# Group maxima spread by fp32r products of diagonals, and the group variances by one fp32r record, in a linear-attention kernel

## The chip, the cores and the metric

The kernel runs on one core of one Trainium2 chip. A core has TensorE (PE: matmuls; PEld: its weight loads), VectorE (DVE), ScalarE (ACT), GpSimd (POOL) and SyncE (SP: the DMA queue here). The metric is the device time of one execution in microseconds (us), lower is better.

## The reference

Sixteen images of 64x64 pixels with 256 channels. Each gets a group norm (32 groups of 8 channels), a linear attention with a softmax of k over the 4096 pixels, an output projection and a residual:

```python
g = x.reshape(16, 64, 64, 32, 8)                          # group norm, no affine part
x_n = (g - mean(g, (1, 2, 4))) / sqrt(var(g, (1, 2, 4)) + 1e-5)
q, k, v = split(einsum('bhwc,cd->bhwd', x_n, W_qkv), 3)   # each to b, channel, pixel
k = softmax(k, axis=-1)                                   # over the 4096 pixels
context = einsum('bdn,ben->bde', k, v)
out = einsum('bde,bdn->ben', context, q)
x + einsum('bhwc,cd->bhwd', out, W_out) + b_out
```

All of it is fp32. The kernel gets fp32 accuracy out of the faster fp32r products by splitting an operand into a high part (rounded to fp32r) and a low part (the rest), and adding the products of both.

## The kernel before

An image is 8 chunks of 512 pixels; CB = 2 halves of 128 channels; x comes in twice, channels on the partitions (xt) and pixels on the partitions (x). The group norm is folded into the weights: wk is scaled by rstd, and the shift of k by the mean drops out of the softmax. For each image: **keys** (k for each chunk, pixels on the partitions, in PSUM; ACT copies it to e_raw, VectorE keeps the running maximum mx of each channel); **exponentials** of k minus a maximum; **gather** (products of the exponentials with x, 8 chunks); **combine** (the 256x256 matrices with wq and wv wo); **emit** (that matrix times xt, plus bias, 8 chunks). TensorE interleaves: in period b it gathers image b, combines it, and then alternates emit of image b with keys of image n = b + 1. Written by hand, each engine's program is a fixed order, unrolled over the 16 images; semaphores (wait_ge, then_inc) tie them together. An engine works in order, so an instruction that waits holds all that is behind it.

The maximum is taken over two **blocks** of four chunks. For each block: `turn_max` (PE transposes mx, channels to the partitions), `block_max` (DVE reduces along the row to m_blk, one maximum for each channel), `spread_max` (PE brings the maxima back as a row on all partitions: the stationary operand is a column of m_blk broadcast to 128x128, the moving one the identity `ident`), `shift` (DVE subtracts that row from e_raw). `block_scales` computes dm, the difference between the block maxima and the whole one, from which ACT makes alpha. Block 0 of image n falls between the keys and emits of period b; block 1 of image b falls behind the first chunks of its own gather.

The statistics of image n are taken by VectorE in period b: BN_STATS on a copy of the input (xs), then `mean_of`: a product with the block matrix grp (1/8 inside a group) gives the group means of the per-channel means, and dev and var2 follow; `stats_var` on PE multiplies var2 by grp, `var_of` adds eps, POOL takes the power -1/2 (rstd), ACT scales wk with it. From image 2 on, both products stand in the gather of the image before, at block 1; image 1's stand later in image 0's gather. POOL makes the low parts: xt_lo and x_lo, each 128x1024 out of two tensors in SBUF. An fp32 product of the program shows in the trace as two records, an fp32r product as one.

The order on PE at block 1, in period b (stats_mean and stats_var for images from 2 on):

```python
gather_high(b, 0)
turn_max(b, 1)
if more and b:
    stats_mean(n)
gather_low(b, 0)
gather_high(b, 1)
spread_max(b, 1)
if more and b:
    stats_var(n)
gather_low(b, 1)
```

Of the kernel before, what the change touches and what calls it, by code (L numbers as in the profile page):

```python
# [31 lines left out]
def build(nc: bass.Bass, xt: bass.AP, xn: bass.AP, w: bass.AP, b_out: bass.AP, out: bass.AP):  # L32
# [11 lines left out]
    with ExitStack() as ctx:  # L44
        def sb(name, shape, dt=F32):
            return ctx.enter_context(nc.sbuf_tensor(name, shape, dt))
# [4 lines left out]
        def sem(name):  # L51
            return ctx.enter_context(nc.semaphore(name))
# [160 lines left out]
        def stats_psum(b, which):  # L213

            return ps_k[:, 0, 0, C + which * CB:C + (which + 1) * CB] if b == 1 else ps_k[:, 1, which, 0:CB]

        def max_psum(b, blk):

            return ps_e if b == 0 and blk == 0 else (ps_g0, ps_k[:, 0])[blk]
# [177 lines left out]
        def _(pe):  # L397
# [50 lines left out]
                last.then_inc(t_ps, 1)  # L448

            def spread_max(b, blk):  # L450

                to = max_psum(b, blk)
                pe.wait_ge(m_blk_ready, b * 2 + (blk + 1))
                for d in range(CB):
                    last = nc.tensor.matmul(to[:, 1, d * P:(d + 1) * P],
                                            m_blk[:, blk, d:d + 1].broadcast_to([P, P]), ident,
                                            start=(d == 0), stop=True, skip_group_check=True)
                last.then_inc(bc_ps, 1)

            def stats_mean(b):  # L460
                pe.wait_ge(mv_ready, b + 1)
                nc.tensor.matmul(stats_psum(b, 0), grp[:], mv[:, :, 0], start=True, stop=True).then_inc(mean_ps, 1)

            def stats_var(b):
                pe.wait_ge(var2_ready, b + 1)
                nc.tensor.matmul(stats_psum(b, 1), grp[:], var2[:], start=True, stop=True).then_inc(var_ps, 1)

            def gather_high(b, j):
                pe.wait_ge(e_hi_ready, b * NCH + (j + 1))
# [115 lines left out]
                emit_low(b, parity, *LATE[i])  # L585

            pe.wait_ge(consts_ready, 5)
            stats_mean(0)
            stats_var(0)
            pe.wait_ge(wvo_loaded, 32)  # L590
# [81 lines left out]
        def _(act):  # L672
# [165 lines left out]
        def _(dve):  # L838
# [19 lines left out]
            def mean_of(b, parity):  # L858
                dve.wait_ge(mean_ps, b + 1)
                nc.vector.tensor_tensor(dev[:], mv[:, :, 0], stats_psum(b, 0), ALU.subtract)  # L860
                nc.vector.tensor_scalar(neg_mean[:, parity, :], stats_psum(b, 0), -1.0, None,
                                        ALU.mult).then_inc(mean_read, 1)
                dve.wait_ge(mean_read, b + 1)
                for c in range(CB):
                    last = nc.vector.tensor_scalar(var2[:, c:c + 1], dev[:, c:c + 1], dev[:, c:c + 1], mv[:, c, 1:2],
                                                   ALU.mult, ALU.add)
                last.then_inc(var2_ready, 1)

            def var_of(b):
                dve.wait_ge(var_ps, b + 1)  # L870
                nc.vector.tensor_scalar(var_eps[:], stats_psum(b, 1), EPS, None, ALU.add).then_inc(var_eps_ready, 1)

            def wk_low(b, parity):
                dve.wait_ge(wk_hi_ready, b + 1)
# [23 lines left out]
            def block_max(b, blk):  # L898
                src = max_psum(b, blk)
                dve.wait_ge(t_ps, b * 2 + (blk + 1))  # L900
                nc.vector.tensor_reduce(m_blk[:, blk, :], src[:, 0, 0:C].rearrange("p (d n) -> p d n", d=CB),
                                        AX_X, ALU.max).then_inc(m_blk_ready, 1)

            def block_scales(b):
                dve.wait_ge(m_blk_ready, b * 2 + 2)
# [147 lines left out]
            def gather_steps(b, parity, more):  # L1053
                n, np_ = b + 1, 1 - parity
                block_max(b, 1)
                if more:
                    mean_of(n, np_)
                block_scales(b)
                mean_bias(b, parity)
                shift(b, 4)  # L1060
                if more:
                    var_of(n)
                e_low(b, 3)
                shift(b, 5)
# [86 lines left out]
```

## Time and profile before

| what | us |
|---|---|
| median of 3 runs | 1215.09 (1214.95 to 1216.85) |
| the profiled execution, its own time | 1214.93 |
| its span, first to last instruction | 1213.2 |
| PE busy | 1190.1 |
| PEld busy (overlaps PE) | 1115.8 |
| DVE busy | 842.1 |
| ACT busy | 840.1 |
| POOL busy | 622.4 |

The rows below come from the one profiled execution. A row of a timeline has the start in us from the span's start, the length in us (of all its xN instructions together), engine, line, operation, and out<-in by the program's names; in brackets the idle time before it and what ended it. Instructions of one engine are pipelined, so their records overlap; the distance between two starts tells what one costs. A name stands for its memory: m_blk is the block maxima, `zero_eye` holds the identity.

### The profile page before, as it was taken

What the parts mean: (1) busy time and instruction counts of PE and PEld (TensorE: products, weight loads), DVE (VectorE), ACT (ScalarE), POOL (GpSimd) and SP (SyncE); (2) the same over time, 40 slices, a digit from 0 to 9 for tenths busy, and PEclk for the clock granted to TensorE, in tenths of its full rate; (3) what the DMA queues carried; (4) which work ended last, traced back from release to release, by engine and by line L of the source; (5) the groups of instructions that cost most, each with busy time, mean ns of one, the idle gap of its engine ahead of it and who ended that gap; (6) DMA issues with size and microseconds to landing.
All of it is one profiled execution on the core that took longest, in us unless ns stands there. A gap on an engine that the chain in (4) does not pass through costs nothing.

```text
span 1213.2 us, 21447 instructions
## 1 busy us (share of the span) xinstructions
PE 1190.1 (98%) x8460; PEld 1115.8 (92%) x8460; DVE 842.1 (69%) x1582; ACT 840.1 (69%) x1140; POOL 622.4 (51%) x288
## 2 busy tenths in 40 slices
PE   4999999999999999999999999999999999999998
PEld 4998999999899998999989999899999989999897
DVE  6877667676776767768776677766767676676551
ACT  5767768677685776757677686776857768577664
POOL 8664564635645355563655636356463564536520
PEclk9999999999999999999999999999999999999999
DMA  9448666576765758666486665867657576573524
GB/s 339 146 167 294 218 235 205 195 269 208 274 203 199 264 172 294 226 206 237 162 301 229 221 227 183 286 209 252 204 201 263 193 278 225 201 252 122 191 74 170
DMA packets 107077, 266.71 MB, mean 220 GB/s; under 512 B 10208, under 2 KB 10208, under 8 KB 106976
## 3 DMA queue, kind: packets, MB, share of 16 engines
q1 hardware_dynamic: 106976, 265.33, 63.5%
q8 instruction: 67, 1.10, 0.4%
q14 instruction: 34, 0.28, 0.1%
HBM read 198.18 MB, written 67.11 MB: 219 GB/s over the span
## 4 chain that ended last, share of the span: by engine, by line
PE 93%; DVE 2%; ACT 1%; POOL 1%; DMA 1%; issue 1%; SPq 0%; DVEq 0%; POOLq 0%; ACTq 0%
PE ps_k L399 29%; PE ps_e L564 19%; PE ps_e L573 10%; PE ps_g L492 5%; PE ps_e L480 5%; PE ps_e L492 5%; PE ps_e L482 5%; PE ps_g L480 4%; PE ps_g L482 4%; PE ps_g L511 1%; PE ps_g L528 1%; PE ps_g L542 1%; PE ps_g L534 1%; POOL x_lo L347 1%; DVE mx L892 1%
## 5 line engine op out<-in xcount | busy, mean ns | idle before, releaser
L341 POOL TENSOR_TENSOR xt_lo<-xt_raw,xt_hi 128x1024 fp32r<-128x1024 f32 x128 | 307.4, 2404 | 434.5 <-ACT xt_hi L676 309.1
L347 POOL TENSOR_TENSOR x_lo<-x_raw,x_hi 128x1024 fp32r<-128x1024 f32 x128 | 281.4, 2216 | 65.6 <-ACT x_hi L681 56.2
L892 DVE TENSOR_TENSOR mx<-ps_k,mx 128x256 f32<-128x256 f32 x480 | 203.3, 424 | 95.8 <-ACT e_raw L685 74.3
L733 ACT ACTIVATE o_stage<-ps_e,bias 128x512 f32<-128x512 f32 x253 | 170.9, 689 | 114.1 <-PE ps_e L573 114.1
L399 PE MATMUL ps_k<-wk_hi,xt_hi 128*128 128x256 f32 x1024 | 207.1, 284 | 1.0 <-DVE mx L892 0.7
L399 PE MATMUL ps_k<-wk_lo,xt_hi 128*128 128x256 f32 x1024 | 205.5, 283 | 0.0
L685 ACT ACTIVATE e_raw<-ps_k 128x512 f32<-128x512 f32 x256 | 141.4, 596 | 87.2 <-PE ps_k L399 87.2
L849 DVE BATCH_NORM_STATS2 bn<-xs 128x6 f32<-128x512 f32 x240 | 154.5, 686 | 40.7 <-DMA xs<-in_xt_dram 39.5
L693 ACT ACTIVATE e_hi<-e_raw 128x1024 fp32r<-128x1024 f32 x128 | 135.1, 1055 | 60.9 <-DVE e_raw L917 33.0
L399 PEld LDWEIGHTS ps_k<-wk_hi,xt_hi 128*128 128x128 f32 x1024 | 163.4, 190 | 8.7 <-issue 1.8
L399 PE MATMUL ps_k<-wk_hi,xt_lo 128*128 128x256 f32 x1024 | 158.2, 283 | 0.0
L399 PEld LDWEIGHTS ps_k<-wk_lo,xt_hi 128*128 128x128 f32 x1024 | 157.4, 189 | 0.0
L564 PE MATMUL ps_e<-xt_hi,acc_hi 128*128 128x512 f32 x474 | 150.3, 398 | 0.0
L573 PE MATMUL ps_e<-xt_hi,u_lo 128*128 128x512 f32 x474 | 150.2, 398 | 0.0
L564 PE MATMUL ps_e<-xt_lo,acc_hi 128*128 128x512 f32 x474 | 148.8, 395 | 0.0
L681 ACT ACTIVATE x_hi<-x_raw 128x1024 fp32r<-128x1024 f32 x128 | 134.5, 1050 | 11.4 <-DMA x_raw<-in_xn_dram 11.2
L676 ACT ACTIVATE xt_hi<-xt_raw 128x1024 fp32r<-128x1024 f32 x128 | 135.0, 1055 | 3.8 <-DMA xt_raw<-in_xt_dram 3.8
L399 PEld LDWEIGHTS ps_k<-wk_hi,xt_lo 128*128 128x128 f32 x1024 | 137.3, 189 | 0.0
L480 PE MATMUL ps_e<-x_hi,e_hi 128*128 128x258 f32 x512 | 125.8, 283 | 0.7 <-POOL x_lo L347 0.7
L482 PE MATMUL ps_e<-x_lo,e_hi 128*128 128x256 f32 x512 | 125.5, 282 | 0.0
L482 PE MATMUL ps_g<-x_lo,e_hi 128*128 128x256 f32 x512 | 124.8, 281 | 0.0
L480 PE MATMUL ps_g<-x_hi,e_hi 128*128 128x258 f32 x512 | 124.8, 282 | 0.0
(129 smaller groups left out, 1992.7 us busy)
## 6 DMA issues: line engine op xcount, KB each, us to landing
xt_raw<-in_xt_dram SPq DMA_DIRECT2D x128, 512.0 KB, 4.3
x_raw<-in_xn_dram SPq DMA_DIRECT2D x128, 512.0 KB, 3.5
out_dram<-o_stage SPq DMA_DIRECT2D x127, 512.0 KB, 4.5
xs<-in_xt_dram SPq DMA_DIRECT2D x240, 256.0 KB, 5.1
w_setup<-in_w_dram SPq DMA_DIRECT2D x2, 256.0 KB, 10.1
out_dram<-o_stage SPq DMA_DIRECT2D x2, 256.0 KB, 2.0
wk<-in_w_dram SPq DMA_DIRECT2D x1, 256.0 KB, 9.9
wq_t<-in_w_dram SPq DMA_DIRECT2D x1, 256.0 KB, 10.9
```

Source lines behind the costliest of these rows:

```text
L341: nc.gpsimd.tensor_tensor(xt_lo[:, s], xt_raw[:, s], xt_hi[:, s].bitcast(F32), ALU.subtract).then_inc(xt_lo_ready, 1)
L347: nc.gpsimd.tensor_tensor(x_lo[:, s], x_raw[:, s], x_hi[:, s, :, 0:C].bitcast(F32), ALU.subtract).then_inc(x_lo_ready, 1)
L399: return nc.tensor.matmul(ps_k[:, j % 2, t // 2, (t % 2) * C:(t % 2 + 1) * C], (xt_hi, xt_lo)[xs_][:, slot(j, parity), c, t * P:(t + 1) * ...
L480: nc.tensor.matmul(ps_g[j // HALF][:, d, 0:C + 2], w_, x_hi[:, j % X_SLOTS, t, :], start=(j % HALF == 0 and t == 0), stop=False, skip_grou ...
L482: nc.tensor.matmul(ps_g[j // HALF][:, d, 0:C], w_, x_lo[:, j % X_SLOTS, t, :], start=False, stop=False, skip_group_check=True)
L564: nc.tensor.matmul(out_psum(b, u, h), hi[:, c, h * P:(h + 1) * P], x_[:, s, c, :], start=(n == 0 and c == 0), stop=False, skip_group_check ...
L573: last = nc.tensor.matmul(out_psum(b, u, h), lo[:, c, h * P:(h + 1) * P], xt_hi[:, s, c, :], start=False, stop=(c == CB - 1), skip_group_c ...
L685: nc.scalar.activation(e_raw[:, j, 2 * h:2 * h + 2, :].rearrange("p t c -> p (t c)"), ps_k[:, j % 2, h, :], ACT.Copy).then_inc(k_out, 1)
L693: nc.scalar.activation(e_hi[:, j % E_SLOTS], e_raw[:, j], ACT.Exp).then_inc(e_hi_ready, 1)
L733: nc.scalar.activation(o_stage[:, u % O_SLOTS, h, :], src, ACT.Identity, bias=bias[:, h:h + 1]).then_inc(o_ready, 1)
L849: nc.vector.bn_stats(bn[:, q % CB, q // CB, :], xs[:, q % S_SLOTS, :]).then_inc(bn_done, 1)
L892: nc.vector.tensor_tensor(mx[:], tile, mx[:], ALU.max).then_inc(max_done, 1)
```

## The change

From image 1 on, the spread multiplies a column of ones (`one_r`, broadcast to 128x128, fp32r) by a diagonal: VectorE builds diag_hi, the identity times m_blk rounded to fp32r, and diag_lo, identity times m_blk minus diag_hi (`block_diag`, right behind `block_max`), and PE adds two products of 256 columns. For the variances from image 1 on, VectorE splits var2 into a high and a low part side by side (var_parts), PE makes one fp32r product of 4 columns, and VectorE adds the two results. Image 0 keeps the fp32 products. grp becomes grp_r, an fp32r copy in the same memory that ACT writes at the start (1/8 and 0 are exact), and its fp32 products read it as fp32. The diagonals use the memory of u_hi, which is needed later in a period.

```diff
@@ tiles
-        grp = sb("grp", [P, P])
+        with nc.sbuf_tensor("grp", [P, P], F32) as grp:
+            pass
+        grp_r = sb("grp_r", [P, P], F32R)
+        one_r = sb("one_r", [P, 1], F32R)
+        var_sum = sb("var_sum", [P, CB])
+        var_parts = sb("var_parts", [P, 2, CB], F32R)
...
+        diag_hi, diag_lo = u_hi[:, 0, :], u_hi[:, 1, :]
@@ PE, spread_max
+                if b == 0:
...
+                else:
+                    pe.wait_ge(diag_hi_ready, (b - 1) * 2 + (blk + 1))
+                    nc.tensor.matmul(to[:, 1, 0:C], one_r[:].broadcast_to([P, P]), diag_hi, start=True, stop=False)
+                    pe.wait_ge(diag_lo_ready, (b - 1) * 2 + (blk + 1))
+                    last = nc.tensor.matmul(to[:, 1, 0:C], one_r[:].broadcast_to([P, P]), diag_lo,
+                                            start=False, stop=True)
@@ PE, stats_var
+                if b == 0:
...
+                else:
+                    pe.wait_ge(var_parts_ready, b)
+                    nc.tensor.matmul(var_psum(b), grp_r[:], var_parts[:].rearrange("p k c -> p (k c)"), start=True,
+                                     stop=True).then_inc(var_ps, 1)
@@ ACT, before its first chunk
+            act.wait_ge(consts_ready, 5)
+            nc.scalar.activation(grp_r[:], grp[:], ACT.Copy).then_inc(grp_r_ready, 1)
+            nc.scalar.activation(one_r[:], one_col[:], ACT.Copy).then_inc(one_r_ready, 1)
@@ DVE, end of mean_of
+                if b > 0:
+                    dve.wait_ge(var2_ready, b + 1)
+                    nc.vector.tensor_copy(var_parts[:, 0, :], var2[:]).then_inc(var_hi_ready, 1)
+                    dve.wait_ge(var_hi_ready, b)
+                    nc.vector.tensor_tensor(var_parts[:, 1, :], var2[:], var_parts[:, 0, :].bitcast(F32),
+                                            ALU.subtract).then_inc(var_parts_ready, 1)
@@ DVE, var_of
+                    nc.vector.tensor_scalar(var_sum[:], sums[:, 0:CB], EPS, None, ALU.add).then_inc(var_sum_ready, 1)
+                    dve.wait_ge(var_sum_ready, b)
+                    nc.vector.tensor_tensor(var_eps[:], sums[:, CB:2 * CB], var_sum[:],
+                                            ALU.add).then_inc(var_eps_ready, 1)
@@ DVE, new
+            def block_diag(b, blk):
+                if b == 0:
+                    return
+                dve.wait_ge(m_blk_ready, b * 2 + (blk + 1))
+                for d in range(CB):
+                    last = nc.vector.tensor_scalar(diag_hi[:, d * P:(d + 1) * P], ident, m_blk[:, blk, d:d + 1], None,
+                                                   ALU.mult)
+                last.then_inc(diag_hi_ready, 1)
+                dve.wait_ge(diag_hi_ready, (b - 1) * 2 + (blk + 1))
+                for d in range(CB):
+                    last = nc.vector.scalar_tensor_tensor(out=diag_lo[:, d * P:(d + 1) * P], in0=ident,
+                                                          scalar=m_blk[:, blk, d:d + 1],
+                                                          in1=diag_hi[:, d * P:(d + 1) * P].bitcast(F32),
+                                                          op0=ALU.mult, op1=ALU.subtract)
+                last.then_inc(diag_lo_ready, 1)
@@ DVE, gather_steps
                 block_max(b, 1)
+                block_diag(b, 1)
                 if more:
                     mean_of(n, np_)
@@ DVE, period
                 block_max(n, 0)
+                block_diag(n, 0)
                 bn_halves(8, 12)
```

PE at block 1 of an image from 1 to 14, behind the last products of gather_high(b, 1); before:

```order
L480 MATMUL ps_g0<-x_hi,e_hi 128x258
L482 MATMUL ps_g0<-x_lo,e_hi 128x256
L455 MATMUL ps_k<-zero_eye,m_blk 128x128 x2
L466 MATMUL ps_k<-var2,grp 128x2
L492 MATMUL ps_g0<-x_hi,e_lo 128x258 x8
```

The same place after the change (the lines of the program have moved: L512 and L514 are the old L480 and L482, L524 the old L492):

```order
L512 MATMUL ps_g0<-x_hi,e_hi 128x258
L514 MATMUL ps_g0<-x_lo,e_hi 128x256
L480 MATMUL ps_k<-u_hi,one_r 128x256
L482 MATMUL ps_k<-u_hi,one_r 128x256
L497 MATMUL ps_k<-var_parts,grp_r 128x4
L524 MATMUL ps_g0<-x_hi,e_lo 128x258 x8
```

The two fp32 products of the spread have become two fp32r products of double width, and the variance product has four columns; nothing else has moved there.

VectorE at the same block 1, from block_max to var_of; before:

```order
L901 TENSOR_REDUCE m_blk<-ps_k 128x2
L860 TENSOR_TENSOR dev<-mv,ps_k 128x2
L861 TENSOR_SCALAR neg_mean<-ps_k 128x2
L865 TENSOR_SCALAR var2<-dev,mv 128x1 x2
L906 TENSOR_REDUCE m_all<-m_blk 128x2
L909 TENSOR_TENSOR dm<-m_blk,m_all 128x4
L961 TENSOR_TENSOR b_mean<-b_col,neg_mean 128x2
L917 TENSOR_TENSOR e_raw<-e_raw,ps_k 128x1024
L871 TENSOR_SCALAR var_eps<-ps_k 128x2
```

After (L952 is the old L901, L897 to L902 the old L860 to L865, u_hi is the diagonals):

```order
L952 TENSOR_REDUCE m_blk<-ps_k 128x2
L960 TENSOR_SCALAR u_hi<-zero_eye,m_blk 128x128 x2
L965 SCALAR_TENSOR_TENSOR u_hi<-zero_eye,m_blk,u_hi 128x128 x2
L897 TENSOR_TENSOR dev<-mv,ps_k 128x2
L898 TENSOR_SCALAR neg_mean<-ps_k 128x2
L902 TENSOR_SCALAR var2<-dev,mv 128x1 x2
L907 CAST var_parts<-var2 128x2
L909 TENSOR_TENSOR var_parts<-var2,var_parts 128x2
L973 TENSOR_REDUCE m_all<-m_blk 128x2
L976 TENSOR_TENSOR dm<-m_blk,m_all 128x4
L1028 TENSOR_TENSOR b_mean<-b_col,neg_mean 128x2
L984 TENSOR_TENSOR e_raw<-e_raw,ps_k 128x1024
```

Four instructions stand between block_max and mean_of, and two more behind var2.

VectorE at block 0, behind the maxima of chunk 3; before:

```order
L892 TENSOR_TENSOR mx<-ps_k,mx 128x256 x4
L901 TENSOR_REDUCE m_blk<-ps_g0 128x2
L849 BN_STATS bn<-xs 128x6 x4
L917 TENSOR_TENSOR e_raw<-e_raw,ps_g0 128x1024
L889 COPY mx<-ps_k 128x256
```

After (L886 is the old L849, L984 the old L917):

```order
L943 TENSOR_TENSOR mx<-ps_k,mx 128x256 x4
L952 TENSOR_REDUCE m_blk<-ps_g0 128x2
L960 TENSOR_SCALAR u_hi<-zero_eye,m_blk 128x128 x2
L965 SCALAR_TENSOR_TENSOR u_hi<-zero_eye,m_blk,u_hi 128x128 x2
L886 BN_STATS bn<-xs 128x6 x4
L984 TENSOR_TENSOR e_raw<-e_raw,ps_g0 128x1024
```

The four instructions of the diagonals stand between block_max and the BN_STATS.

## Rows read from the trace of the kernel before

**Rows 1.** Page, busy time; then one image's window: us, busy us and instructions by engine, PEclk.

```profile
PE 1190.1 (98%) x8460; PEld 1115.8 (92%) x8460; DVE 842.1 (69%) x1582; ACT 840.1 (69%) x1140; POOL 622.4 (51%) x288
...
201.00:275.00 74.00, 74.00 (x531) 69.53 (x530) 52.77 (x100) 52.22 (x71) 38.35 (x18) 1.00 0.66 228
```

**Rows 2.** Waits of PE between 60 and 1150 us: total, times, longest.

```profile
PE ps_e L480 <- POOL x_lo L347: 0.7, 2, 0.4
```

**Rows 3.** Timeline of weight loads, block 1 (start, length, us).

```profile
498.64 0.53 PEld L455 LDWEIGHTS ps_k<-zero_eye,m_blk 128*128 128x128 f32 x4
499.09 0.30 PEld L466 LDWEIGHTS ps_k<-var,grp 128*128 128x128 f32 x2
499.31 1.02 PEld L492 LDWEIGHTS ps_g<-x_hi,e_lo 128*128 128x128 f32 x8
```

**Rows 4.** The same at block 0 of the next image.

```profile
546.12 1.02 PEld L399 LDWEIGHTS ps_k<-wk_hi,xt_lo 128*128 128x128 f32 x8
547.07 0.53 PEld L455 LDWEIGHTS ps_g<-zero_eye,m_blk 128*128 128x128 f32 x4
547.52 0.30 PEld L564 LDWEIGHTS ps_e<-xt_hi,acc_hi 128*128 128x128 f32 x2
```

**Rows 5.** Groups by form, VectorE: busy us, mean ns, idle before.

```profile
L876 DVE SCALAR_TENSOR_TENSOR wk_lo<-wk,rstd,wk_hi 128x256 fp32r<-128x256 f32 x32 | 13.9, 478 | 0.3 <-ACT wk_hi L708 0.3
```

**Rows 6.** Timeline of VectorE at block 1.

```profile
495.87 0.42 DVE L901 TENSOR_REDUCE m_blk<-ps_k 128x2 f32<-128x256 f32 x1 [1.71 <-PE ps_k L447]
496.21 0.15 DVE L860 TENSOR_TENSOR dev<-mv,ps_k 128x2 f32<-128x2 f32 x1
...
496.47 0.46 DVE L865 TENSOR_SCALAR var<-dev,mv 128x1 f32<-128x1 f32 x2
...
497.02 0.83 DVE L909 TENSOR_TENSOR dm<-m_blk,m_all 128x4 f32<-128x4 f32 x1
...
499.40 1.22 DVE L917 TENSOR_TENSOR e_raw<-e_raw,ps_k 128x1024 f32<-128x1024 f32 x1 [1.47 <-PE ps_k L455]
```

**Rows 7.** Timeline of VectorE at block 0.

```profile
544.54 0.42 DVE L901 TENSOR_REDUCE m_blk<-ps_g 128x2 f32<-128x256 f32 x1 [1.00 <-PE ps_g L447]
546.04 2.58 DVE L849 BATCH_NORM_STATS2 bn<-xs 128x6 f32<-128x512 f32 x4 [1.07 <-DMA xs<-in_xt_dram]
```

**Rows 8.** The tile dm: ns min/median/max over 16 images.

```profile
L909 DVE TENSOR_TENSOR dm<-m_blk,m_all x16: 161/833/849, 52.0 to 1158.7; 128x4 f32<-128x4 f32 x16
```

**Rows 9.** Timeline of GpSimd around block 1.

```profile
495.45 2.39 POOL L341 TENSOR_TENSOR xt_lo<-xt_raw,xt_hi 128x1024 fp32r<-128x1024 f32 x1 [7.59 <-ACT xt_hi L676]
500.77 1.60 POOL L357 TENSOR_TENSOR rstd<-var_eps,neg_half 128x2 f32<-128x2 f32 x1 [2.93 <-DVE var_eps L871]
```

**Rows 10.** Image 0: VectorE, then GpSimd.

```profile
55.31 2.79 DVE L924 TENSOR_TENSOR e_lo<-e_raw,e_hi 128x1024 fp32r<-128x1024 f32 x1
...
54.60 2.41 POOL L341 TENSOR_TENSOR xt_lo<-xt_raw,xt_hi 128x1024 fp32r<-128x1024 f32 x1
56.97 3.19 POOL L347 TENSOR_TENSOR x_lo<-x_raw,x_hi 128x1024 fp32r<-128x1024 f32 x1
```

**Rows 11.** Image 15: VectorE, then weight loads of PE.

```profile
1155.16 1.87 DVE L892 TENSOR_TENSOR mx<-ps_k,mx 128x256 f32<-128x256 f32 x4 [2.48 <-ACT e_raw L685]
...
1157.08 0.20 PEld L447 LDWEIGHTS ps_k<-zero_eye,mx 128*128 128x128 f32 x2 [0.47 <-DVE mx L892]
```

**Rows 12.** The start: ACT, then GpSimd's last constant.

```profile
4.25 1.06 ACT L676 ACTIVATE xt_hi<-xt_raw 128x1024 fp32r<-128x1024 f32 x1 [2.17 <-DMA xt_raw<-in_xt_dram]
...
2.58 0.40 POOL L333 TENSOR_SCALAR_AFFINE_SELECT grp<-grp 128x128 f32<-128x128 f32 x1
```

**Rows 13.** Timeline of GpSimd around block 0.

```profile
543.15 2.40 POOL L341 TENSOR_TENSOR xt_lo<-xt_raw,xt_hi 128x1024 fp32r<-128x1024 f32 x1 [3.19 <-ACT xt_hi L676]
546.04 2.40 POOL L341 TENSOR_TENSOR xt_lo<-xt_raw,xt_hi 128x1024 fp32r<-128x1024 f32 x1 [0.48 <-ACT xt_hi L676]
```

More of the change, by code:

```diff
@@ L153, in build @@
         var2_ready = sem("var2_ready")
+        grp_r_ready = sem("grp_r_ready")
+        var_hi_ready = sem("var_hi_ready")
+        var_sum_ready = sem("var_sum_ready")
+        var_parts_ready = sem("var_parts_ready")
         var_ps = sem("var_ps")
@@ L167, in build @@
         m_blk_ready = sem("m_blk_ready")
+        diag_hi_ready = sem("diag_hi_ready")
+        diag_lo_ready = sem("diag_lo_ready")
+        one_r_ready = sem("one_r_ready")
         bc_ps = sem("bc_ps")
@@ L215, in stats_psum, with var_psum @@
             return ps_k[:, 0, 0, C + which * CB:C + (which + 1) * CB] if b == 1 else ps_k[:, 1, which, 0:CB]
+        def var_psum(b):
+            return ps_k[:, 0, 0, C + CB:C + 3 * CB] if b == 1 else ps_k[:, 1, 1, 0:2 * CB]
         def max_psum(b, blk):
@@ L452, in spread_max @@
                 to = max_psum(b, blk)
[L453 to L457, printed above, removed]
+                if b == 0:
+                    pe.wait_ge(m_blk_ready, blk + 1)
+                    for d in range(CB):
+                        last = nc.tensor.matmul(to[:, 1, d * P:(d + 1) * P],
+                                                m_blk[:, blk, d:d + 1].broadcast_to([P, P]), ident,
+                                                start=(d == 0), stop=True, skip_group_check=True)
+                else:
[4 more added lines that the diff above has]
+                                            start=False, stop=True)
                 last.then_inc(bc_ps, 1)
@@ L461, in stats_mean @@
                 pe.wait_ge(mv_ready, b + 1)
-                nc.tensor.matmul(stats_psum(b, 0), grp[:], mv[:, :, 0], start=True, stop=True).then_inc(mean_ps, 1)
+                nc.tensor.matmul(stats_psum(b, 0), grp_r[:].bitcast(F32), mv[:, :, 0], start=True, stop=True).then_inc(mean_ps, 1)
             def stats_var(b):
-                pe.wait_ge(var2_ready, b + 1)
-                nc.tensor.matmul(stats_psum(b, 1), grp[:], var2[:], start=True, stop=True).then_inc(var_ps, 1)
+                if b == 0:
+                    pe.wait_ge(var2_ready, 1)
+                    nc.tensor.matmul(stats_psum(b, 1), grp_r[:].bitcast(F32), var2[:], start=True,
+                                     stop=True).then_inc(var_ps, 1)
+                else:
+                    pe.wait_ge(var_parts_ready, b)
+                    nc.tensor.matmul(var_psum(b), grp_r[:], var_parts[:].rearrange("p k c -> p (k c)"), start=True,
+                                     stop=True).then_inc(var_ps, 1)
             def gather_high(b, j):
@@ L587, in _ @@
             pe.wait_ge(consts_ready, 5)
+            pe.wait_ge(grp_r_ready, 1)
             stats_mean(0)
@@ L609, in _ @@
             keys(0, 0, 4)
+            pe.wait_ge(one_r_ready, 1)
             turn_max(0, 0)
@@ L867, in mean_of @@
                 last.then_inc(var2_ready, 1)
+                if b > 0:
[4 more added lines that the diff above has]
+                                            ALU.subtract).then_inc(var_parts_ready, 1)
             def var_of(b):
                 dve.wait_ge(var_ps, b + 1)
-                nc.vector.tensor_scalar(var_eps[:], stats_psum(b, 1), EPS, None, ALU.add).then_inc(var_eps_ready, 1)
+                if b == 0:
+                    nc.vector.tensor_scalar(var_eps[:], stats_psum(b, 1), EPS, None,
+                                            ALU.add).then_inc(var_eps_ready, 1)
+                else:
+                    sums = var_psum(b)
+                    nc.vector.tensor_scalar(var_sum[:], sums[:, 0:CB], EPS, None, ALU.add).then_inc(var_sum_ready, 1)
+                    dve.wait_ge(var_sum_ready, b)
+                    nc.vector.tensor_tensor(var_eps[:], sums[:, CB:2 * CB], var_sum[:],
+                                            ALU.add).then_inc(var_eps_ready, 1)
             def wk_low(b, parity):
@@ L902, in block_max @@
                                         AX_X, ALU.max).then_inc(m_blk_ready, 1)
+            def block_diag(b, blk):
+                if b == 0:
+                    return
[5 more added lines that the diff above has]
+                dve.wait_ge(diag_hi_ready, (b - 1) * 2 + (blk + 1))
+                for d in range(CB):
+                    last = nc.vector.scalar_tensor_tensor(out=diag_lo[:, d * P:(d + 1) * P], in0=ident,
[3 more added lines that the diff above has]
+                last.then_inc(diag_lo_ready, 1)
             def block_scales(b):
```

## Prediction

> **What bounds the kernel now.** I read the page's busy line first: TensorE is busy for 98% of the span, its weight loads for 92%, no other engine for more than 69% [rows 1]. The windows say it again: from 201 to 275 us, one image long, TensorE is busy 74.00 of 74.00 us at a granted clock of 1.00 [rows 1]. Then the waits: from 60 to 1150 us it waited 0.7 us in all, none of it for VectorE [rows 2]. So a record taken from TensorE comes off the end one for one, and so does a wait put before it, on 14 or 15 images in a row. The reader should look at two places of an image, here image 6's gather (its block 1) and image 7's keys (its block 0), and then at VectorE and GpSimd beside them.
>
> **What TensorE saves.** Busy records overlap, so I price by the distance of weight-load starts. Block 1's spread starts at 498.64, the variance product at 499.09, the next work at 499.31: 0.45 us for the spread's four fp32 records and 0.22 for the variance's two [rows 3]. At block 0 the spread takes 547.07 to 547.52, 0.45 again, and eight fp32r records of 256 columns before it take 546.12 to 547.07, 0.12 each [rows 4]. The new spread is two such records: 0.24, saving 0.21. The new variance product is one record with 4 columns. No row has an fp32r record so narrow; the two-column fp32 ones take 0.11 each and the 256-column fp32r ones 0.12, so I take 0.12, which saves 0.10 (bounds: 0.05 and 0.22 for the record, 2 us over the run). In all: block 0 of images 1 to 15, 15 x 0.21 = 3.15; block 1 of images 1 to 15, 15 x 0.21 = 3.15; 15 variances, 15 x 0.10 = 1.5. Sum 7.8 us, 0.64% of the run.
>
> **What VectorE gets.** Per spread two tensor_scalar and two scalar_tensor_tensor of 128x128; per variance a copy and a subtraction of 128x2, and an addition behind the product. The 256-wide three-operand form takes 0.478 us [rows 5]. A 1024-wide row takes 1.22 and a 256-wide 0.42 [rows 6], so 128 elements cost 0.133, and a 128-wide op is 0.345; the next may start 0.08 before its end, as 496.21 follows a row that ends at 496.29 [rows 6], so one every 0.26. An op that waits for its predecessor's semaphore starts 0.04 after its end.
>
> *Block 0.* m_blk is there at 544.96; VectorE then waits 1.07 us for a DMA [rows 7]. The four ops take 545.00 to 546.24, while TensorE asks for the second diagonal at 547.19. Hidden, with 0.95 us to spare; without that cover it would cost what is missing, 15 times. The next BN_STATS slip by 0.1 to 0.2 us, and nothing on TensorE waits for them.
>
> *Block 1.* Here a second engine matters. dm, four elements wide, both inputs in SBUF, starts at 497.02 and takes 0.83 us [rows 6], against 0.161 in the last image [rows 8]. It ends at 497.85; GpSimd's xt_lo runs from 495.45 to 497.84 [rows 9]. In image 0, e_lo with two SBUF inputs takes 2.79 us instead of 1.22, and GpSimd's op of 54.60 ends at 57.01, right before the e_lo's last 1.1 us [rows 10]. So a VectorE op with two SBUF inputs is held until a running GpSimd op ends. The Trainium skill says this too (page "SBUF — State Buffer", section "Who interferes with whom"); these rows agree. Before the change only dm stood in that stretch, and nobody on TensorE needed it. Now the diagonals stand there, and mean_of stands behind them on VectorE:
> - m_blk at 496.29; the two tensor_scalar from 496.33 to 496.93, one SBUF tensor each, not held;
> - the first scalar_tensor_tensor (identity and diag_hi, both SBUF) starts at 496.97, is held to 497.84, ends at 498.00; the second ends at 498.26. The spread wants it at 498.64 + 0.12 = 498.76: in time;
> - dev starts at 498.18 instead of 496.21 [rows 6], 1.97 us late; var2, which was ready at 496.93, is at 498.90; copy and subtraction, 0.15 each as the 128x2 row of 496.21, with 0.04 ahead of each: var_parts ready at 499.28;
> - TensorE would load for the variance at 498.64 + 0.24 = 498.88. A load starts 0.05 after what it waited for (maximum done at 1157.03, load at 1157.08 [rows 11]), so at 499.33: 0.45 us lost, and behind it stand all the gather's products.
> That happens where GpSimd has an xt_lo in the stretch and a variance follows: images 1 to 14, 14 x 0.45 = 6.3 us. With the fp32 variance product var2 at 498.90 would be 0.07 us late for the earlier load; the two extra small ops are 0.38 of the 0.45. In image 0 the mean stands far from any diagonal, and the two ops cost nothing there; in image 15 GpSimd is idle and no variance follows.
>
> Edits that I cost at nothing: two small ACT copies at the start, which need GpSimd's last constant (2.98) and come before the first chunk's copy at 4.25, for which ACT sat idle 2.17 us [rows 12], cover 1.2 us; the added addition on VectorE before var_eps, 0.2 us, whose only taker is rstd, which wk_high wants after the gather's last exponentials; dm and shift(b, 4), which end up at about 499.4 and 499.5 against 499.40 for the shift before [rows 6].
>
> **Sum.** 1214.93 (the profiled run, whose span is 1213.2) - 7.8 + 6.3 = 1213.4 us. The median of the three runs, 1215.09, is 0.16 above the profiled one; I let it be inside the rounding. What a measurement of this kernel can tell from no change is about 0.2%, 2.4 us. Bounds for the 128-wide op are 0.15 (the 128x2 row) and 0.478 (the 256-wide one): the hold eats the early ones, and the last two move var_parts by -0.2 to +0.26 us, times 14: 1210.6 to 1217.
>
> **The rivals.**
> - *Nothing is held* (7.8 us kept). dm and e_lo are tensor_tensor; no row has a scalar_tensor_tensor in a GpSimd stretch. Unheld, the diagonals end at 497.57, var_parts at 498.6, before 498.83. 1214.9 - 7.8 = 1207.1. Against it: the inputs are two SBUF tensors, as dm's are.
> - *The tensor_scalars are held too* (slower). var2 is a tensor_scalar on SBUF in the same stretch, and it is not held: 0.46 for two in 496.47 to 496.93 [rows 6]. But it is one element wide, and none of the rows has a wide one. If the first waits for 497.84, both pairs follow after it: tensor_scalars until 498.12 to 498.25, second scalar_tensor_tensor until 498.76 to 498.89, var_parts at 499.80, load at 499.85, 0.97 us lost. 14 x 0.97 = 13.6: 1214.9 - 7.8 + 13.6 = 1220.7. It decides as soon as the loss passes 7.8 / 14 = 0.56 us.
> - *GpSimd slips in at block 0.* GpSimd ends an xt_lo at 545.55 and starts the next at 546.04 [rows 13]. If the tensor_scalars are held to 545.55, the second scalar_tensor_tensor starts at about 546.13, behind GpSimd's 546.04. A waiting engine gets in between two ops of the other: GpSimd's x_lo of 56.97 takes 3.19 us, because e_lo had waited for the op before it and went first [rows 10]. Then the second diagonal ends at about 548.64 and TensorE loads at 548.69 instead of 547.19: 1.50 us, 15 times, 22.5 on top of 1220.7: 1243. It needs the previous rival and a race lost by about 0.1 us.
> The Trainium skill speaks against the change here (page "VectorE: DVE Perf Modes", section "The perf-mode tier table", with "Who interferes with whom" of the page "SBUF — State Buffer"): a tensor_scalar from SBUF to SBUF runs in a mode with both ports even in fp32, and in it contends with GpSimd. By that rule the second rival is the forecast; no row here shows such an op. The rows that I have show a tensor_scalar that is not held.
>
> **How the numbers follow.** Held scalar_tensor_tensors alone: 0.32, the likeliest, 1213.4. Nothing held: 0.23. The tensor_scalars held as well: 0.22. GpSimd slipping in: 0.20. Something else, such as a lost cover at the start: 0.03, slower. The range leaves out only the fourth and this last, in part: 1206 to 1223, where 1206 is 1207.1 with a variance record of 0.05, and 1223 is 1220.7 with 256-wide prices. Faster by over 0.2% (below 1212.7): 0.22 of the unheld case and 0.12 of the likeliest, 0.34. Within: 0.18 of the likeliest, 0.03 of the second rival, 0.01: 0.22. Slower: 0.19, 0.20, 0.03 and 0.02 of the likeliest: 0.44. The likeliest case's own range is 1210.6 to 1217, mostly below no change.
>
> **What would show it.** In the changed kernel's trace: weight loads of the spread 0.24 us apart from what follows; in images 1 to 14 a TensorE wait on var_parts of 0.4 to 0.5 us (none: first rival; near 1: second); the first scalar_tensor_tensor of block 1 longer than 1 us and the tensor_scalars at 0.35 (or the first of them at 1.6); at block 0 the four ops done before 546.3 in this image's time, and no TensorE wait on u_hi. A wait on u_hi at block 0 is the third rival. I am wrong altogether if a broadcast stationary fp32r operand takes another pace than 0.12 us, or if GpSimd's xt_lo moves out of the stretch.

## The result

| what | us |
|---|---|
| before, median of 4 runs | 1215.97 (1214.95 to 1217.30) |
| after, median of 4 runs | 1244.38 (1242.48 to 1245.16) |
| ratio | 1.0231, 95% interval 1.0213 to 1.0248 |
| the profiled execution of after, its own time; its span | 1243.68; 1242.0 |

The change made the kernel 2.3% slower. The granted clock of TensorE was 1.00 throughout in both.

### The profile after

The busy line of the page and the image of [rows 1] again:

```profile
PE 1190.5 (96%) x8385; PEld 1108.5 (89%) x8385; DVE 921.4 (74%) x1747; ACT 840.5 (68%) x1142; POOL 622.0 (50%) x288
...
201.00:275.00 74.00, 72.07 (x517) 67.39 (x516) 56.57 (x107) 50.86 (x70) 38.30 (x17) 1.00 0.65 221
```

TensorE has 75 products fewer and the span is 28.8 us longer: in the window from 201 to 275 us it is busy for 72.07 of 74.00 us, so it stands still for 1.9 us where [rows 1] had none. The waits of weight loads, 60 to 1170 us (total, times, longest), name the places:

```profile
PEld ps_g L482 <- DVE u_hi L965: 19.7, 14, 1.4
PEld ps_k L497 <- DVE var_parts L909: 11.7, 14, 0.8
PEld ps_e L596 <- ACT o_stage L767: 4.2, 14, 0.4
```

Before, TensorE's products waited 0.7 us from 60 to 1150 us [rows 2], and its weight loads 1.0 us. Block 1 of image 6 first; [rows 6] and [rows 9] are its counterpart. VectorE's timeline:

```profile
507.90 0.42 DVE L952 TENSOR_REDUCE m_blk<-ps_k 128x2 f32<-128x256 f32 x1 [1.65 <-PE ps_k L465]
508.36 1.81 DVE L960 TENSOR_SCALAR u_hi<-zero_eye,m_blk 128x128 fp32r<-128x128 f32 x2
510.20 0.61 DVE L965 SCALAR_TENSOR_TENSOR u_hi<-zero_eye,m_blk,u_hi 128x128 fp32r<-128x128 f32 x2
510.74 0.15 DVE L897 TENSOR_TENSOR dev<-mv,ps_k 128x2 f32<-128x2 f32 x1
...
511.68 0.16 DVE L909 TENSOR_TENSOR var_parts<-var,var_parts 128x2 fp32r<-128x2 f32 x1
...
511.94 0.16 DVE L976 TENSOR_TENSOR dm<-m_blk,m_all 128x4 f32<-128x4 f32 x1
```

GpSimd's:

```profile
507.50 2.39 POOL L359 TENSOR_TENSOR xt_lo<-xt_raw,xt_hi 128x1024 fp32r<-128x1024 f32 x1 [7.19 <-ACT xt_hi L710]
```

And the weight loads, to be laid beside [rows 3]:

```profile
510.69 0.19 PEld L480 LDWEIGHTS ps_k<-u_hi,one_r 128*128 128x128 f32 x1
510.87 0.18 PEld L482 LDWEIGHTS ps_k<-u_hi,one_r 128*128 128x128 f32 x1
511.90 0.19 PEld L497 LDWEIGHTS ps_k<-var_parts,grp_r 128*128 128x128 f32 x1 [0.84 <-DVE var_parts L909]
512.00 1.03 PEld L524 LDWEIGHTS ps_g<-x_hi,e_lo 128*128 128x128 f32 x8
```

The two tensor_scalar take 1.81 us together. GpSimd's xt_lo ends at 507.50 + 2.39 = 509.89; the pair ends at 510.17, which is 0.28 us later, the time of one unheld tensor_scalar. So the first of them was held, and dm, which was held in [rows 6], now stands behind and takes 0.16. Everything behind the pair is late. The variance load comes at 511.90 where it could have come 0.12 after the load before, at 510.99: 0.91 us lost. That load before was itself 0.06 late: the second diagonal is ready at 510.20 + 0.61 = 510.81 and is loaded at 510.87, where 510.69 + 0.12 = 510.81 was possible. In all 0.97 us.

Block 0 of image 7, whose counterpart is [rows 7]; VectorE:

```profile
557.61 0.84 DVE L960 TENSOR_SCALAR u_hi<-zero_eye,m_blk 128x128 fp32r<-128x128 f32 x2
558.49 2.73 DVE L965 SCALAR_TENSOR_TENSOR u_hi<-zero_eye,m_blk,u_hi 128x128 fp32r<-128x128 f32 x2
561.15 2.46 DVE L886 BATCH_NORM_STATS2 bn<-xs 128x6 f32<-128x512 f32 x4
```

GpSimd ([rows 13] has the same two instructions):

```profile
555.78 2.39 POOL L359 TENSOR_TENSOR xt_lo<-xt_raw,xt_hi 128x1024 fp32r<-128x1024 f32 x1 [3.18 <-ACT xt_hi L710]
558.65 2.42 POOL L359 TENSOR_TENSOR xt_lo<-xt_raw,xt_hi 128x1024 fp32r<-128x1024 f32 x1 [0.47 <-ACT xt_hi L710]
```

Weight loads ([rows 4]):

```profile
559.68 0.19 PEld L480 LDWEIGHTS ps_g<-u_hi,one_r 128*128 128x128 f32 x1
561.28 0.19 PEld L482 LDWEIGHTS ps_g<-u_hi,one_r 128*128 128x128 f32 x1 [1.41 <-DVE u_hi L965]
...
567.39 0.30 PEld L596 LDWEIGHTS ps_e<-xt_hi,acc_hi 128*128 128x128 f32 x2 [0.29 <-ACT o_stage L767]
```

The first tensor_scalar is held from 557.61 to 558.17, the end of GpSimd's xt_lo. The first scalar_tensor_tensor starts at 558.49; the second could start 0.26 later, at 558.75, but GpSimd's next xt_lo is issued at 558.65 and goes first. So the second diagonal is ready only at 561.22, after GpSimd's end at 561.07. TensorE loads it at 561.28 instead of 559.80: 1.48 us lost. The shift behind is late as well, ACT's exponential and output copy after it, and TensorE waits another 0.3 us for o_stage.

Of the 15 images with a diagonal, image 9 alone has no wait on u_hi. The tensor_scalars of its block 0 are held as in the others (0.84 us for the two), but there GpSimd's next xt_lo comes only 0.47 us after the first scalar_tensor_tensor has started, not 0.16:

```profile
710.41 0.62 DVE L965 SCALAR_TENSOR_TENSOR u_hi<-zero_eye,m_blk,u_hi 128x128 fp32r<-128x128 f32 x2
710.88 2.40 POOL L359 TENSOR_TENSOR xt_lo<-xt_raw,xt_hi 128x1024 fp32r<-128x1024 f32 x1 [0.78 <-ACT xt_hi L710]
```

The two scalar_tensor_tensor take 0.62 us, and the two loads stand 0.12 apart (711.60, 711.72). With the same work on VectorE, GpSimd's start alone decides.

The tile u_hi (min/median/max ns) has the longest of each hold in the run:

```profile
L960 DVE TENSOR_SCALAR u_hi<-zero_eye,m_blk x60: 271/283/1609, 101.7 to 1187.7; 128x128 fp32r<-128x128 f32 x60
L965 DVE SCALAR_TENSOR_TENSOR u_hi<-zero_eye,m_blk,u_hi x60: 344/352/2462, 102.6 to 1188.3; 128x128 fp32r<-128x128 f32 x60
```

**The account.** Each of the two losses stands there 14 times, of the same size within 0.02 us: 14 x 0.97 = 13.6 (block 1 of images 1 to 14) and 14 x 1.48 = 20.7 (block 0 of images 1 to 15 without 9); o_stage adds 4.2: 38.5 us lost. With the forecast saving of 7.8 that is +30.7 against a span that grew by 28.8. Experiment 4 finds some 2 us more that the changed kernel gains elsewhere.

### The profile page after: what moved, and what is told of

The parts are those of the page before. It is cut to its first block, busy times and chain, and to the rows that moved or that the text cites. A ratio compares the mean times of both kernels' runs of the same rounds, so it can differ in the third digit from the quotient of the medians.

```text
span 1242.0 us, 21465 instructions
## 1 busy us (share of the span) xinstructions
PE 1190.5 (96%) x8385; PEld 1108.5 (89%) x8385; DVE 921.4 (74%) x1747; ACT 840.5 (68%) x1142; POOL 622.0 (50%) x288
## 4 chain that ended last, share of the span: by engine, by line
PE 78%; DVE 15%; ACT 3%; issue 2%; DMA 1%; POOL 1%; SPq 0%; DVEq 0%; POOLq 0%; ACTq 0%
PE ps_k L417 21%; PE ps_e L596 17%; PE ps_e L605 9%; PE ps_e L512 5%; PE ps_e L524 5%; PE ps_e L514 5%; DVE u_hi L965 4%; PE ps_g L524 4%; PE ps_g L512 4%; PE ps_g L514 4%; DVE u_hi L960 3%; DVE bn L886 3%; DVE e_raw L984 2%; ACT e_raw L733 1%; PE ps_g L543 1%
## 5 line engine op out<-in xcount | busy, mean ns | idle before, releaser
L886 DVE BATCH_NORM_STATS2 bn<-xs 128x6 f32<-128x512 f32 x240 | 152.5, 681 | 25.7 <-DMA xs<-in_xt_dram 24.7
L512 PE MATMUL ps_e<-x_hi,e_hi 128*128 128x258 f32 x512 | 125.7, 283 | 0.3 <-POOL x_lo L365 0.3
L514 PE MATMUL ps_e<-x_lo,e_hi 128*128 128x256 f32 x512 | 125.4, 282 | 0.0
L512 PE MATMUL ps_g<-x_hi,e_hi 128*128 128x258 f32 x512 | 124.8, 282 | 0.0
L514 PE MATMUL ps_g<-x_lo,e_hi 128*128 128x256 f32 x512 | 124.7, 281 | 0.0
```

Source lines behind the costliest of these rows:

```text
L512: nc.tensor.matmul(ps_g[j // HALF][:, d, 0:C + 2], w_, x_hi[:, j % X_SLOTS, t, :], start=(j % HALF == 0 and t == 0), stop=False, skip_grou ...
L514: nc.tensor.matmul(ps_g[j // HALF][:, d, 0:C], w_, x_lo[:, j % X_SLOTS, t, :], start=False, stop=False, skip_group_check=True)
L886: nc.vector.bn_stats(bn[:, q % CB, q // CB, :], xs[:, q % S_SLOTS, :]).then_inc(bn_done, 1)
```

## The experiments

The theory: two holds by GpSimd's xt_lo. At block 1 it holds the tensor_scalars, so that var_parts is late; at block 0 it holds them too, and the next xt_lo gets in between the two scalar_tensor_tensor. The rivals: that the waits come from VectorE's added work alone, with GpSimd only beside it; or that the fp32r products cost something of their own.

### 1. One half of the change alone

**spread_only** has the diagonals and keeps the variance in fp32; the split in mean_of and the addition in var_of are gone too:

```diff
...
-                if b == 0:
-                    pe.wait_ge(var2_ready, 1)
+                if True:
+                    pe.wait_ge(var2_ready, b + 1)
                     nc.tensor.matmul(stats_psum(b, 1), grp_r[:].bitcast(F32), var2[:], start=True,
...
```

> The changed kernel with the variances taken back to one fp32 product each (no split of var2, no addition behind it). Theory (GpSimd's xt_lo holds VectorE at both blocks): block 0 stays as it is, 1.48 us lost per image; at block 1 TensorE now waits for var2 instead of var_parts, about 0.50 us instead of 0.91 on 14 images. 1243.7 - 5.7 + 1.5 = about 1239.5. Rival (the variance split is what costs, not the hold): back to 1207 to 1215.

Measured: 1240.61 us (1238.60 to 1242.64), ratio 1.0207 (1.0192 to 1.0222). Its waits of weight loads, 1 to 1170 us:

```profile
PEld ps_g L482 <- DVE u_hi L965: 19.7, 14, 1.4
...
PEld ps_k L493 <- DVE var L902: 7.1, 15, 0.9
PEld ps_e L596 <- ACT o_stage L767: 3.9, 14, 0.4
```

The diagonals bring most of the loss, 25 of the 28 us. Even without the two small ops of the split the variance is late, by 0.44 us in each of 14 images (the 15th wait, 0.9 us, is at the start).

**var_only** keeps the fp32 spreads (spread_max has its fp32 branch in every image) and has the split variance:

```diff
...
             def block_diag(b, blk):
-                if b == 0:
+                if True:
                     return
```

> The changed kernel with all spreads taken back to fp32 products (no diagonals). Theory: dev and var2 come as early as before the change, the copy into var_parts is held until GpSimd's xt_lo ends, and var_parts is ready about 1 us before TensorE wants it: no wait, and only the 15 shorter variance products remain, about 1.5 us saved against the kernel before: 1213.4. Rival (the split of var2 costs TensorE a wait by itself): above 1216, with a TensorE wait on var_parts.

Measured: 1211.63 us (1210.26 to 1215.66), ratio 0.997 (0.9961 to 0.9979). No wait on var_parts, as expected, but a gain of 3.8 us where 1.5 was estimated. The weight loads at the place of the product show only 0.11 us of it in an image:

```profile
496.98 0.53 PEld L474 LDWEIGHTS ps_k<-zero_eye,m_blk 128*128 128x128 f32 x4
497.43 0.19 PEld L497 LDWEIGHTS ps_k<-var_parts,grp_r 128*128 128x128 f32 x1
497.54 1.01 PEld L524 LDWEIGHTS ps_g<-x_hi,e_lo 128*128 128x128 f32 x8
```

0.11 for the product against 0.22 in [rows 3]. The tile var_parts shows the hold that the expectation had, and that the prediction had not:

```profile
L907 DVE CAST var_parts<-var x15: 168/926/929, 63.1 to 1084.1; 128x2 fp32r<-128x2 f32 x15
```

A copy of two elements is held as well (0.93 us instead of 0.17). TensorE does not wait for it here.

### 2. GpSimd held back

If GpSimd is the cause, an xt_lo that starts after the diagonals takes the waits away, with the same work on every engine. **pool_after_0** does it at block 0 (chunk 5's xt_lo waits for the diagonals), **pool_after_1** at block 1:

```diff
@@ pool_after_0
                     for j in range(3, NCH):
+                        if j == 5:
+                            pool.wait_ge(diag_lo_ready, b * 2 + 1)
                         xt_low(n, np_, j)
@@ pool_after_1
                 if more:
+                    if b:
+                        pool.wait_ge(diag_lo_ready, (b - 1) * 2 + 2)
                     xt_low(n, np_, 0)
```

> The changed kernel, and GpSimd waits for the second diagonal of block 0 before its xt_lo of chunk 5, so that it can't get in between the two scalar_tensor_tensor. Theory (slip-in): the TensorE wait on u_hi at block 0, 1.48 us, and the one on o_stage behind it, 0.3 us, both go; block 1 stays. 1243.7 - 14 x 1.78 = about 1218.8; the tensor_scalars of block 0 are still held by the xt_lo before. Rival (block 0 is late because VectorE has too much to do there): no change, 1243.

> The changed kernel, and GpSimd waits for the second diagonal of block 1 before its xt_lo of the next image's chunk 0. Theory (hold): nothing is held at block 1, the diagonals are done 1.3 us after m_blk, var_parts 2.3 us after it, and TensorE does not wait for it: 14 x 0.91 = 12.7 us back, 1231. Rival (the six added instructions take too long by themselves): a wait on var_parts stays, above 1237.

pool_after_0: 1219.41 us (1218.56 to 1219.95), ratio 1.0034 (1.0021 to 1.0046). Of the change's waits one is left:

```profile
PEld ps_k L499 <- DVE var_parts L911: 11.8, 14, 0.8
```

The waits on u_hi and on o_stage are gone, 25 us with them, and the longest scalar_tensor_tensor is 353 ns instead of 2462. So the slip-in at block 0 is shown, and o_stage goes with it. The slip-in is not the only way to an o_stage wait: in the changed kernel image 9, which has no slip-in, still has one of 0.4 us. There the BN_STATS, and with them the shift, had waited 0.58 us for a DMA.

pool_after_1 missed: 1249.66 us (1249.28 to 1250.14), ratio 1.0282 (1.0266 to 1.0297), slower than the change itself, where 1231 was expected. Its VectorE at block 1:

```profile
510.45 0.48 DVE L962 TENSOR_SCALAR u_hi<-zero_eye,m_blk 128x128 fp32r<-128x128 f32 x2
510.97 0.61 DVE L967 SCALAR_TENSOR_TENSOR u_hi<-zero_eye,m_blk,u_hi 128x128 fp32r<-128x128 f32 x2
...
511.76 0.46 DVE L904 TENSOR_SCALAR var<-dev,mv 128x1 f32<-128x1 f32 x2
512.25 1.84 DVE L909 CAST var_parts<-var 128x2 fp32r<-128x2 f32 x1
```

and GpSimd:

```profile
511.67 2.40 POOL L359 TENSOR_TENSOR xt_lo<-xt_raw,xt_hi 128x1024 fp32r<-128x1024 f32 x1 [9.24 <-DVE u_hi L967]
```

The diagonals are no longer held, as the theory says, but GpSimd now starts ahead of the copy of the variance, which is held to 511.67 + 2.40 = 514.07. The wait on var_parts grew from 0.84 to 1.26 us in an image. Which op is held depends on where the window of the other engine falls; I had moved the window onto the next op.

**pool_after_dm** therefore lets xt_lo wait at block 1 for dm, the last of the small ops, with the wait of pool_after_0 at block 0:

```diff
                 if more:
+                    if b:
+                        pool.wait_ge(dm_ready, b + 1)
                     xt_low(n, np_, 0)
```

> The changed kernel, and GpSimd waits for the second diagonal at block 0 (before xt_lo of chunk 5) and for dm at block 1 (before xt_lo of chunk 0), so that none of VectorE's added instructions and not the dm behind them meets a running GpSimd op, except the tensor_scalars of block 0. Theory (the hold is all that is wrong): no TensorE wait on u_hi or var_parts; the variance record is worth 3.8 us as the run with it alone showed, the spreads 30 x 0.21 = 6.3: 1215.4 - 3.8 - 6.3 = about 1205.5. Rival (GpSimd now starts some 3 us later and xt_lo, rstd and x_lo behind it come too late for the gather): above 1209, with TensorE waits on x_lo or wk_lo.

Measured: 1206.33 us (1205.71 to 1207.88), ratio 0.9925 (0.9909 to 0.9942). It beats both kernels. VectorE, block 1:

```profile
495.53 0.48 DVE L964 TENSOR_SCALAR u_hi<-zero_eye,m_blk 128x128 fp32r<-128x128 f32 x2
496.05 0.61 DVE L969 SCALAR_TENSOR_TENSOR u_hi<-zero_eye,m_blk,u_hi 128x128 fp32r<-128x128 f32 x2
```

and its weight loads:

```profile
497.85 0.19 PEld L484 LDWEIGHTS ps_k<-u_hi,one_r 128*128 128x128 f32 x1
497.97 0.19 PEld L486 LDWEIGHTS ps_k<-u_hi,one_r 128*128 128x128 f32 x1
498.08 0.19 PEld L501 LDWEIGHTS ps_k<-var_parts,grp_r 128*128 128x128 f32 x1
498.20 0.90 PEld L528 LDWEIGHTS ps_g<-x_hi,e_lo 128*128 128x128 f32 x7
```

Spread and variance take 0.35 us here, 0.67 in [rows 3]. TensorE waits for neither. So the fp32r products have no cost of their own; the second of the rivals falls. So does the first: the added work on VectorE is all there, and TensorE never waits for it. At block 0 the first tensor_scalar is still held, 0.65 us at the longest, and the slack there covers it.

### 3. Other ways around the hold

**hi_on_act** leaves GpSimd alone and has ScalarE write diag_hi; only the scalar_tensor_tensors are left to be held, which is the prediction's likeliest case:

```diff
@@ VectorE: diag_hi's tensor_scalars go
...
@@ ScalarE, ahead of exps(b, 3) and of chunk 5's xt_high
...
+                for d in range(CB):
+                    last = nc.scalar.activation(diag_hi[:, d * P:(d + 1) * P], ident, ACT.Copy,
+                                                scale=m_blk[:, blk, d:d + 1])
+                last.then_inc(diag_hi_ready, 1)
```

> The changed kernel with diag_hi made by ScalarE (two activations with m_blk as the scale) in place of VectorE's two tensor_scalar; diag_lo stays on VectorE, GpSimd as it is. Theory: without the held tensor_scalars, block 0's scalar_tensor_tensor run while GpSimd is between two ops, no wait there; at block 1 the first of them is still held to the end of xt_lo, and var_parts is about 0.45 us late, as the prediction's likeliest case had it: 1215.4 - 10.1 + 6.3 = 1211.6. Rival (ScalarE's two copies delay its exponentials or key copies enough to stall TensorE): above 1216.

Measured: 1212.16 us (1211.11 to 1215.48), ratio 0.9975 (0.9966 to 0.9984). The first scalar_tensor_tensor is held, there is no wait on u_hi, and the wait on var_parts is 0.4 us (beside it TensorE waits 1.5 us for o_stage, in four images together):

```profile
498.12 1.14 DVE L972 SCALAR_TENSOR_TENSOR u_hi<-zero_eye,m_blk,u_hi 128x128 fp32r<-128x128 f32 x2 [0.83 <-ACT u_hi L740]
```

```profile
PEld ps_k L497 <- DVE var_parts L920: 5.5, 14, 0.4
```

**block1_fp32** keeps the fp32 spread at block 1, the diagonals at block 0 with pool_after_0's wait there:

```diff
...
             def block_diag(b, blk):
-                if b == 0:
+                if b == 0 or blk == 1:
                     return
```

> The changed kernel with fp32 spreads at block 1, diagonals at block 0 alone, the fp32r variance record, and GpSimd waiting for the second diagonal at block 0. Theory: no wait anywhere; 1215.4 - 3.8 (variances) - 15 x 0.21 (spreads of block 0) = 1208.4. Rival (a tensor_scalar pair that is held at block 0 makes the second diagonal late even without the slip-in): a TensorE wait on u_hi, 1212 or more.

Measured: 1208.76 us (1208.32 to 1210.35), ratio 0.9946 (0.9932 to 0.9961), and no wait on u_hi or var_parts.

### 4. Where the gain of var_only comes from

**both_fp32** has neither part: spreads and variances are fp32 in every image, and only the surroundings of the change are left (the new tiles, the fp32r copy of grp, ScalarE's two copies at the start). It joins the edits of spread_only and var_only. **pool_after_dm_var32** is pool_after_dm with spread_only's edit.

> Only what surrounds the two parts is left of the change: the tiles, the fp32r copy of the block matrix in the memory of the old one, the two ScalarE copies at the start. Spreads and variances are the fp32 products of before. The run with the variances alone came out 3.8 us under before, of which the records at the place of the product show some 1.7 (0.12 us in each of 14 images). If the other 2 us belong to the fp32r variance products: this kernel takes the time of before, 1215.7 us, within 0.2%. If they belong to what surrounds them (tiles, copies, lines): about 1213.6 us, and the 24 products of the keys read 2.84 us here too, not 2.88.

> The best kernel so far (GpSimd waits for the diagonals at block 0 and for dm at block 1, 1206.3 us) with the variances as fp32 products again. If the variance part is worth the 3.8 us that it gave alone: 1210.1 us. If it is worth only what its records show, 0.12 us x 14 = 1.7: 1208.0 us. Either way no wait of TensorE on the diagonals or on var.

both_fp32: 1212.34 us (1211.33 to 1214.65, 11 runs) against 1215.10 of before beside it (15 runs), ratio 0.998 (0.9972 to 0.9989). pool_after_dm_var32: 1206.79 us (1205.36 to 1207.48), ratio 0.9927 (0.9913 to 0.9940); the expectation, 1208.0 or 1210.1, missed by over 1 us. So some 2.4 us of var_only's gain belong to neither product. The fp32r variance itself comes out at 0.1% in one pair (0.998 to 0.997) and 0.02% in the other (0.9927 to 0.9925); the intervals separate neither from nothing.

The traces measure finer than the times. The distance from turn_max's loads at block 1 of image 6 to those of image 7 is the time of one image, without the start and the end of the run. Before, 73.93 us:

```profile
495.34 0.25 PEld L447 LDWEIGHTS ps_k<-zero_eye,mx 128*128 128x128 f32 x2
569.27 0.25 PEld L447 LDWEIGHTS ps_k<-zero_eye,mx 128*128 128x128 f32 x2
```

both_fp32, 73.71:

```profile
495.07 0.25 PEld L465 LDWEIGHTS ps_k<-zero_eye,mx 128*128 128x128 f32 x2
568.78 0.25 PEld L465 LDWEIGHTS ps_k<-zero_eye,mx 128*128 128x128 f32 x2
```

The same distance in other runs, each within 0.04 us of the median over its images: var_only 73.60, pool_after_dm_var32 73.30, pool_after_dm 73.13, the change 75.98. So the surroundings are worth 0.22 us in an image, the variance 0.11 (against both_fp32) or 0.17 (between the last two kernels), and the two spreads together 0.41 (pool_after_dm_var32 against both_fp32, with GpSimd's waits, which no run has without the diagonals). The change loses 2.85 us in an image against pool_after_dm; 0.97, 1.48 and 0.3 make 2.75 of it.

Before's weight loads of one step of keys and emit, 479.25 to 484.93, take 5.68 us:

```profile
479.25 0.31 PEld L564 LDWEIGHTS ps_e<-xt_hi,acc_hi 128*128 128x128 f32 x2
479.62 0.42 PEld L564 LDWEIGHTS ps_e<-xt_lo,acc_hi 128*128 128x128 f32 x2
...
484.93 0.31 PEld L564 LDWEIGHTS ps_e<-xt_hi,acc_hi 128*128 128x128 f32 x2
```

In both_fp32 the same step takes 5.64:

```profile
479.09 0.31 PEld L596 LDWEIGHTS ps_e<-xt_hi,acc_hi 128*128 128x128 f32 x2
479.44 0.42 PEld L596 LDWEIGHTS ps_e<-xt_lo,acc_hi 128*128 128x128 f32 x2
...
484.73 0.31 PEld L596 LDWEIGHTS ps_e<-xt_hi,acc_hi 128*128 128x128 f32 x2
```

Hundredths of a microsecond in the same products, in a part of the program that the change doesn't touch, add up to the 0.22 us of an image. The profiled spans differ by 2.1 us, less than 15 x 0.22 = 3.3, for two reasons that can be seen: both_fp32 reaches its first block 1 1.0 us later, and one of its images takes 0.6 us longer. Why the products are quicker is open: the addresses of tiles and the place of the code both moved, and no run separates them.

## Why the prediction was wrong

It gave 1213.4 us, 1206 to 1223, and a chance of 0.44 that the kernel gets slower. The time came out at 1244, outside the range; the fourth case, GpSimd slipping in (0.20, 1243 us), is what happened.

- **What TensorE saves: right.** 0.12 us for a 256-column fp32r record with a broadcast column of ones, 0.11 to 0.12 for the four-column one (pool_after_dm's loads: 0.35 for all three, forecast 0.36). In an image the two spreads save 0.41 us where the sum had 0.42, and the variance 0.11 to 0.17 where it had 0.10. In times the spreads bring 5.6 us by the medians (1212.34 - 1206.79) or 6.4 by the ratios (0.998 - 0.9927), where the sum had 6.3; this pair of kernels differs by GpSimd's waits too. The variance's 1.5 us is too small for the times to confirm.
- **The cost of the VectorE ops: right.** A scalar_tensor_tensor of 128 takes 0.352 us against 0.345 estimated; the tensor_scalar is quicker, 0.283. Two of them take 0.48 us, two scalar_tensor_tensor 0.61.
- **The step that failed** is the first of block 1: "the two tensor_scalar from 496.33 to 496.93, one SBUF tensor each, not held". They are held: the first took 1.61 us. With that the term for TensorE's waits, 14 x 0.45 = 6.3 us, became 38.5 us. I had only var2's row, 0.46 us for two in GpSimd's stretch, and carried it from one element to 128, though the prediction itself says that it is one element wide. That row is right (pool_after_1 has it again, 0.46 us for two at 511.76, inside GpSimd's op) and says nothing on a wide op. I gave the held tensor_scalars 0.42 in all, 0.22 and 0.20, and should have given them the greater part. The rule of the Trainium skill stood beside it (page "VectorE: DVE Perf Modes", section "The perf-mode tier table"; page "SBUF — State Buffer", section "Who interferes with whom"): a tensor_scalar from SBUF to SBUF in a mode with both ports contends with GpSimd. The trace now agrees: 1.61 us when held. It agrees for the fp32 to fp32r copy too (0.93 and 1.84 us).
- **Second rival, block 1: right in mechanism and size.** It had the first tensor_scalar held to the end of xt_lo and 0.97 us lost, counted from the first load of the spread; 0.97 was lost.
- **Third rival, block 0: right in mechanism and size.** "A race lost by about 0.1 us": GpSimd was 0.10 us ahead of the second scalar_tensor_tensor (558.65 against 558.75). 1.50 us forecast, 1.48 lost. Once the tensor_scalars are held, this race is lost too in 14 images of 15; it was not a case of 0.20 beside one of 0.22 but nearly the same case. The range was cut between the two. That the total, 1243, meets the measured 1244 so closely is in part luck: it leaves out the 4.2 us of o_stage, counts one image too many, and leaves out what the surroundings gained.
- **The likeliest case was right about what it described.** hi_on_act realizes it: scalar_tensor_tensor with two SBUF inputs held (0.89 us the longest), 0.39 us of wait per image against 0.45. Its time, 1212.2 against 1213.4, has the gain of the surroundings in it, which the 1213.4 has not.
- **Edits costed at nothing.** ACT's two copies are done at 3.42 us, ahead of its first chunk (4.17), and TensorE nowhere waits for var_eps, so neither edit costs anything that shows. Still, TensorE's first load comes later in every kernel that carries the new start: at 15.84 us here and at 16.1 to 16.6 in the others' traces, against 15.30 before. VectorE's first BN_STATS wait 0.7 to 1.5 us there for a chunk's DMA and did not before. Why the DMA is later no run tells, and before has one trace only. Two terms were missing: 4.2 us for o_stage behind the late shift of block 0, and the 2 to 3 us gained by the surroundings. With these and the measured losses, 1214.93 - 7.8 - 2.1 + 38.5 = 1243.5 against the profiled 1243.68.

## What to carry to other kernels

Before putting VectorE work into a stretch, lay GpSimd's timeline over it. In the stretches shown here, VectorE ops of three kinds that came while GpSimd's xt_lo ran waited for its end, and so did everything behind them: a tensor_scalar of 128x128 and a copy of 128x2, each from SBUF to SBUF, and ops with two SBUF inputs (dm, scalar_tensor_tensor). The longest wait was 2.1 us. A tensor_scalar of 128x1 did not wait, so the narrowest rows of a trace don't price the wide op. Where GpSimd has slack, letting it start after the *last* short op can be worth more than the faster product: its two waits, one at each block, make 38 us between this change and pool_after_dm, where the products saved some 8. A wait placed a few ops too early, ahead of the copy of the variance, made the kernel slower still.

## What the runs showed that I had not expected

- The prediction had no hold for a copy of 128x2 from fp32 to fp32r (0.926 us in var_only, where the expectation before the run had it; 1.84 in pool_after_1), while two tensor_scalar of 128x1 right ahead of the latter, also inside GpSimd's op, are not held (0.46 us at 511.76).
- The hold is decided by which engine is first, instruction by instruction: in pool_after_1 the diagonals, ahead of GpSimd's start, ran free (0.48 and 0.61 us), and the copy behind it was held. GpSimd can enter between two ops of VectorE that follow each other (558.65, ahead of the second scalar_tensor_tensor), and 0.3 us decide: in image 9 it came that much later, and nothing was lost.
- 0.2% came from the surroundings of the change alone, in 11 and 15 runs. Small parts of a change have to be measured against that kernel, not against the one before.
